# A decoder layer in float32 on one core: eight heads' products with the values in one bank, and a new order of steps

## The chip, the cores and the metric

The kernel runs on one core of one Trainium2 chip. The core has the engines PE (TensorE, matrix products and transposes), ACT (ScalarE), DVE (VectorE) and POOL (GpSimd), each with its own instruction stream, and SP (SyncE), which here issues most DMA transfers. The engines meet only at semaphores. The metric is the device time of one execution in microseconds (us).

## The reference

One decoder layer for 16 sequences of 128 tokens and 128 features, 16 heads of 8 features (`HD = 8`). Cut to what matters:

```python
# self-attention, with relative positions
attn = softmax((einsum('bhqd,bhkd->bhqk', q, k) + einsum('bhqd,qkd->bhqk', q, rk2)) / scale)
w1 = einsum('bhqk,bhkd->bhqd', attn, v)          # products with the values
w2 = einsum('bhqk,qkd->bhqd', attn, rv2)         # products with relative values
x = layernorm(x + (w1 + w2) @ Wo.T + bo)
# causal cross-attention on ctx_1024: weights @ v per head, Wo, residual, layernorm
# feed-forward: a shared expert and 8 experts (top 2 of 8, all computed and weighted), residual, layernorm
```

## The kernel before

The 16 sequences are worked in four chunks of four. For a chunk the kernel runs a list of steps. `SCHEDULE` is a text of words such as `0pv.1`: chunk 0, step `pv`, part 1. Every engine walks the same list `ORDER` in its own loop and picks from it what it has to do, so the text sets the order on each engine, on SP's queue too.

The steps of self-attention: `load` and `loadc` (input DMAs), `xT` (transpose the input), `q`, `k`, `v` (projections), `st_q`, `st_k` (the projections, split into three bf16 parts, are written to DRAM by `spread_parts` and come back stacked by head), `bias` x8 (relative-position scores, copied by ACT into the array `ST`), `p1` x8 (scores; DVE adds them to `ST` and takes maxima), `m` x2 (the row shift from the maxima, sent into the stacked queries by small DMAs), `p2` x8 (DVE subtracts the shift, ACT takes the exponential), `pv` x4 (products with the values), `w2` x4 (products with the relative values), `pvT` x4 and `w2T` x4 (back to tokens on rows), `X` (divide by the row sum), `XT`, `o`, `ln`. Cross-attention has `cT`, `ck`, `cv`, `x1T`, `cq`, `c1` x8, `cm` x2, `c2` x8, `cpv` x4, `cpvT` x4, `cX`, `cXT`, `co`, `cln`. The feed-forward part has `x2T`, `r`, `g`, `up` x18, `dn` x9, `fln`. `lrv` and `lex` load the relative values and the experts' weights once.

PSUM: steps in `S_STEPS` alternate between two double banks `ps_s`; all others, in `F_STEPS`, take the four single banks `ps_f` in turn (`take_f`, which waits until the step four uses earlier is released), and one semaphore `f_full` counts them.

The products with the values: one `pv` step does four heads. Each head's weights are 128 keys by 9 columns (8 values and a column of ones, which gives the row sum). Four heads sit in four column groups of 32 of the array (`tile_position=(0, j * QD)`), so an output bank of 128 rows holds 4 x 9 used rows. ACT copies the bank to `OT` (L818), PE transposes it in four pieces (`pvT`, L581), ACT copies the 9 columns of each head to `X` (L833).

At the start (lines 334 to 360) SP issues the loads of chunk 0, the weights, biases and the context. PE transposes chunk 0 (`xT`), the weights and the biases; the projections `q`, `k`, `v` of chunk 0 each wait for `wt_sb` at 3, by which all of self-attention's weights and the bias column are in place.

Of the kernel before, what the change touches and what calls it, by code (L numbers as in the profile page):

```python
# [98 lines left out]
2up.12 3cpvT.2 3cpv.3 2up.13 3cpvT.3 2dn.6 3cXT 2up.14 3co 2up.15 3cln 2up.16 2dn.7 2up.17 3x2T 3r 3up.0 3up.1
3up.2 2dn.8 3up.3 3g 3up.4 2fln 3up.5 3dn.0 3up.6 3dn.1 3dn.2 3up.7 3up.8 3up.9 3dn.3 3up.10 3up.11 3up.12 3dn.4  # L100
3dn.5 3up.13 3up.14 3up.15 3up.16 3up.17 3dn.6 3dn.7 3dn.8 3fln
# [17 lines left out]
def build(nc, x, ctx, sw, cw, rel_k, rel_v, router_w, router_b, sw1, sb1, sw2, sb2,  # L119
# [8 lines left out]
    F_USES = [s for s in ORDER if s[1] in F_STEPS]  # L128
# [6 lines left out]
    OT_USES = [s for s in ORDER if s[1] in ("pv", "cpv")]  # L135

    st = ExitStack()
    with st:
# [34 lines left out]
        VA = [sb(f"VA{i}", [P, NB, H, HD + 1]) for i in range(2)]  # L173
# [64 lines left out]
        stacked = {k: sem(f"stacked_{k}") for k in ("q", "k", "ck", "cq")}  # L238
        va_ready = [sem(f"va_ready{i}") for i in range(2)]
# [34 lines left out]
        def released(s):  # L274
# [9 lines left out]
                "pv": lambda: (ot_ready[0], NQ * ch + t + 1), "cpv": lambda: (ot_ready[1], NQ * ch + t + 1),  # L284
                "w2": lambda: (ow_ready, NQ * ch + t + 1),
                "pvT": lambda: (xu_ready[0], NQ * ch + t + 1), "cpvT": lambda: (xu_ready[1], NQ * ch + t + 1),
# [25 lines left out]

        def done_f(e, s):

            e.wait_ge(f_full, F_USE[s] + 1)
            return ps_f[F_USE[s] % 4]
# [14 lines left out]
        N_E = 10  # L331
# [3 lines left out]
        def _(sp):  # L335
# [23 lines left out]
            def load_relative_values():  # L359
# [739 lines left out]
```

## Time and profile before

| | |
|---|---|
| median of 3 runs | 450.4 us (450.26 to 450.72) |
| profiled execution | 451.89 us, of which the span is 450.1 us |
| PE busy | 378.3 us, 84% of the span |
| DVE busy | 303.4 us, 67% |
| ACT busy | 228.3 us, 51% |
| POOL busy | 80.0 us, 18% |
| mean granted clock of PE | 0.942 of full speed |

The profiled execution's own time is 1.8 us longer than its span, and 1.5 us longer than the median of the timed runs. "Busy" is the time in which at least one instruction of the engine runs. Matmuls are pipelined, so the mean duration of one is much longer than its share of a dense stream; what a matmul costs in such a stream is read from the length of a stretch divided by its count.

### The profile page before, as it was taken

To read this page: it belongs to the slowest core of one execution; us is meant where nothing else is said; L and a number is where in the kernel's file an instruction comes from. 1 tells how busy PE (TensorE), PEld (TensorE's weight loads), DVE (VectorE), ACT (ScalarE), POOL (GpSimd) and SP (SyncE) were. 2 spreads that over 40 slices of the span, in tenths; PEclk is the share of its full clock that TensorE was granted. 3 is DMA by queue.
4 is the path that set the end of the run, shared out by engine and by line. 5 is a ranking of instruction groups with operands and counts; after the bars stand their busy time and mean duration, and the time that the engine had idled before them with its cause. 6 is when DMAs were issued, how large, how long until landed. Compare 5 with 4: busy or idle time off the path is not lost.

```text
span 450.1 us, 11284 instructions
## 1 busy us (share of the span) xinstructions
PE 378.3 (84%) x4714; PEld 285.1 (63%) x4729; DVE 303.4 (67%) x630; ACT 228.3 (51%) x329; POOL 80.0 (18%) x92
## 2 busy tenths in 40 slices
PE   2556366974789999999999999999998989899992
PEld 1345234763566797767687976776685757566672
DVE  4246984469987679998775889998549476056324
ACT  2343046560069875326877853469944315844330
POOL 8910000020044012011131120003311202411001
PEclk9987559996989999999999999999999999999997
DMA  3261028724101360400112703010200310000100
GB/s 93 73 183 39 4 51 248 202 71 128 28 4 41 108 178 1 128 4 4 39 39 82 214 4 106 4 37 4 75 3 2 100 31 6 1 1 0 25 1 23
DMA packets 29420, 26.87 MB, mean 60 GB/s; under 512 B 12673, under 2 KB 27962, under 8 KB 28602
## 3 DMA queue, kind: packets, MB, share of 16 engines
q1 hardware_dynamic: 26042, 25.86, 20.7%
q8 instruction: 38, 0.62, 0.6%
q10 hardware_dynamic: 3136, 0.27, 0.5%
q14 instruction: 12, 0.10, 0.1%
q0 software_dynamic: 192, 0.03, 0.0%
HBM read 18.38 MB, written 7.35 MB: 57 GB/s over the span
## 4 chain that ended last, share of the span: by engine, by line
PE 54%; DVE 17%; DMA 10%; issue 6%; ACT 5%; SPq 5%; POOL 1%; POOLq 0%; DVEq 0%; ACTq 0%
PE ps_f L725 9%; PE ps_s L547 9%; PE ps_f L714 8%; PE ps_f L573 6%; PE ps_f L581 4%; DMA parts_by_head<-part 3%; PE ps_f L677 3%; PE ps_f L520 3%; DMA QS<-parts_by_head 3%; DVE ST L943 3%; PE ps_s L540 3%; DVE MX L946 3%; PE ps_s L556 2%; PE ps_f L526 2%; PE ps_s L636 2%
## 5 line engine op out<-in xcount | busy, mean ns | idle before, releaser
L547 PE MATMUL ps_s<-QS,KS 125*128 125x128 bf16 (+1 forms) x768 | 79.5, 249 | 11.9 <-DVE ST L943 6.6
L547 PEld LDWEIGHTS ps_s<-QS,KS 125*128 125x128 bf16 (+1 forms) x768 | 65.1, 106 | 34.6 <-DVE ST L943 9.0
L846 ACT ACTIVATE HT<-ps_f,hb 128x512 f32<-128x512 f32 x72 | 48.3, 688 | 74.0 <-PE ps_f L714 44.3
L725 PEld LDWEIGHTS ps_f<-w,HT 128*128 128x128 f32 x576 | 68.8, 192 | 8.1 <-issue 6.0
L725 PE MATMUL ps_f<-w,HT 128*128 128x128 f32 x576 | 72.1, 276 | 0.1
L714 PE MATMUL ps_f<-x2T,w 128*128 128x512 f32 x144 | 70.8, 602 | 1.4 <-DVE acc L1056 1.0
L488 POOL TENSOR_SCALAR_AFFINE_SELECT PC<-PC 128x1024 f32<-128x1024 f32 x32 | 34.8, 1094 | 142.2 <-ACT PC L810 142.2
L1060 DVE SCALAR_TENSOR_TENSOR acc<-ps_f,gw,acc 128x128 f32<-128x128 f32 x128 | 35.7, 341 | 21.8 <-PE ps_f L725 21.5
L810 ACT ACTIVATE PC<-ps_s 128x1024 f32<-128x1024 f32 x32 | 32.2, 1024 | 33.4 <-PE ps_s L547 30.1
L803 ACT ACTIVATE ST<-ST 128x1024 f32<-128x1024 f32 x32 | 33.9, 1061 | 28.0 <-DVE ST L974 27.6
L943 DVE TENSOR_TENSOR ST<-ps_s,ST 128x1024 f32<-128x1024 f32 x32 | 38.6, 1207 | 11.0 <-PE ps_s L547 10.9
L974 DVE TENSOR_TENSOR ST<-ps_s,ST 128x1024 f32<-128x1024 f32 x32 | 38.2, 1216 | 8.6 <-PE ps_s L556 8.2
L950 DVE TRANSPOSE_TENSOR_REDUCE MX<-ps_s 128x32 f32<-128x1024 f32 x32 | 38.7, 1232 | 3.8 <-PE ps_s L547 3.6
L946 DVE TRANSPOSE_TENSOR_REDUCE MX<-ST 128x32 f32<-128x1024 f32 x32 | 39.8, 1245 | 1.1
L494 POOL TENSOR_TENSOR ve<-mv,epst 128x4 f32<-128x4 f32 x12 | 2.4, 202 | 197.1 <-DVE mv L890 197.1
L714 PEld LDWEIGHTS ps_f<-x2T,w 128*128 128x128 f32 x144 | 24.1, 191 | 16.3 <-issue 13.9
L799 ACT COPY ST<-ps_s 128x1024 f32<-128x1024 f32 x32 | 30.9, 1025 | 6.9 <-PE ps_s L636 6.9
L540 PE MATMUL ps_s<-maskT,identb 128*128 128x512 bf16 x64 | 25.8, 402 | 8.7 <-DMA QS<-parts_by_head 5.8
L922 DVE SCALAR_TENSOR_TENSOR rest<-ps_f,bcol,part 128x512 f32<-128x512 f32 x16 | 11.9, 743 | 22.0 <-ACT part L789 22.0
L636 PE MATMUL ps_s<-QS,RK 125*128 125x64 bf16 x512 | 20.5, 197 | 5.9 <-issue 3.7
L636 PEld LDWEIGHTS ps_s<-QS,RK 125*128 125x128 bf16 x512 | 18.9, 101 | 7.9 <-issue 4.4
L556 PE MATMUL ps_s<-QS,onesr 128*128 128x512 bf16 x49 | 17.4, 422 | 6.9 <-DMA QS<-MP 4.3
(118 smaller groups left out, 525.2 us busy)
## 6 DMA issues: line engine op xcount, KB each, us to landing
parts_by_head<-part SPq DMA_DIRECT2D x16, 384.0 KB, 2.6
QS<-parts_by_head SPq DMA_DIRECT2D x24, 256.0 KB, 3.8
KS<-parts_by_head SPq DMA_DIRECT2D x24, 256.0 KB, 4.3
xin<-in_x SPq DMA_DIRECT2D x16, 64.0 KB, 2.7
cin<-in_ctx SPq DMA_DIRECT2D x4, 256.0 KB, 5.0
w<-in_L_ffn_rw SPq DMA_DIRECT2D x1, 1024.0 KB
out_x<-acc SPq DMA_DIRECT2D x16, 64.0 KB, 1.8
QS<-MP SPq DMA_DIRECT2D x32, 8.0 KB, 2.1
```

Of the source, the lines that this page charges most:

```text
L488: nc.gpsimd.affine_select(out=w, in_=w, compare_op=ALU.is_ge, fill=0.0, base=0, pattern=[[0, HB_TILE], [1, S]], channel_multiplier=-1).the ...
L540: nc.tensor.matmul(ps[:, half * BANK:(half + 1) * BANK], identb[:, :], maskT[:, :, :].broadcast_to([P, 4, S]), start=True, stop=False, ski ...
L547: last = nc.tensor.matmul(ps[:, o:o + S], KS[a][0:kd, c:c + S], queries(a, kd, h, j), start=not masked and j == 0, stop=j == NB - 1, skip_ ...
L636: last = nc.tensor.matmul(ps[:, j * HB:(j + 1) * HB], RK[0:KZ, S - 1 - q:2 * S - 1 - q], qs_q[:, :, q, :], start=True, stop=True)
L714: nc.tensor.matmul(ps[:, :], w1[:, e, f * P:(f + 1) * P], x2T[:, :], start=True, stop=True).then_inc(f_full, 1)
L725: last = nc.tensor.matmul(ps[:, b * E:(b + 1) * E], HT[n % 2][:, f, b * S:(b + 1) * S], w2[:, e, f, :], start=f == 0, stop=f == NF - 1 and ...
L846: nc.scalar.activation(HT[n % 2][:, f, :], ps[:, :], ACT.Gelu, bias=hb[:, e, f:f + 1]).then_inc(ht_ready, 1)
L943: nc.vector.tensor_tensor(by_bank(w), ps[:, :].rearrange("p (c b q) -> p c q b", b=2, q=S), by_bank(w), ALU.add).then_inc(sum_ready, 1)
L946: nc.vector.tensor_reduce(MX[0][:, t * 32:(t + 1) * 32], w.rearrange("p c (g i) -> p c g i", i=QD), AXIS.X, ALU.max, apply_transpose=True) ...
L950: nc.vector.tensor_reduce(MX[1][:, t * 32:(t + 1) * 32], ps[:, :].rearrange("p (c i) -> p c i", i=QD), AXIS.X, ALU.max, apply_transpose=Tr ...
L974: nc.vector.tensor_tensor(w, ps[:, :].rearrange("p (c i) -> p c i", i=ST_PAIR), w, ALU.add).then_inc(sc_ready, 1)
L1060: last = nc.vector.scalar_tensor_tensor(acc[:, b, :], ps[:, b * E:(b + 1) * E], gw[ch % 2][:, b, t - 1:t], acc[:, b, :], ALU.mult, ALU.add)
```

## The change

Two `pv` steps (four heads each) now share one output bank. A head's weights become 18 columns: for the first step of a pair the 9 real columns and 9 zeros, for the second 9 zeros and the 9 real columns. The second step adds into the same rows, so that each column group holds two heads. To this end `VA` is laid out with 9 zeros between the heads' 9 columns, and is filled with zeros once. The bank is taken by the first step only; ACT copies it once per pair; there are two `pvT` steps per chunk instead of four, and ACT copies each to `X` in two pieces. The same holds for `cpv` and `cpvT`. The products are counted by semaphores of their own (`pv_done`).

The experts' weights are loaded in pieces of half a tensor (`lup.0`, `lup.1`, `ldn.0`, `ldn.1`, and `lsm` for the small ones) at earlier places of the list, the relative values are extended in DRAM by a step `ext` of its own, the projections `q` and `k` of chunk 0 wait for `wt_sb` at 1 and `v` at 2, and DVE's wait for the bias rows stands at the first `v`. The list of steps is another one.

```diff
@@ SCHEDULE (its first line, of 34)
-0xT 1xT 0load 1load 0loadc 0q 0st_q 0k 0v 0st_k 0wts 0cT 0ck 0cv 0bias.0 ...
+0xT 0load 0loadc 0q 1load 0st_q 0k 0wts 0st_k 0cT 0v 0ck 0ext 1xT 0cv 0bias.0 ...
@@
-    F_USES = [s for s in ORDER if s[1] in F_STEPS]
+    F_USES = [s for s in ORDER if s[1] in F_STEPS and not (s[1] in ("pv", "cpv") and s[2] % 2)]
-        VA = [sb(f"VA{i}", [P, NB, H, HD + 1]) for i in range(2)]
+        VA = [sb(f"VA{i}", [P, VW + NB * H * 2 * VW]) for i in range(2)]
+        VA_head = [va[:, VW:VW + NB * H * 2 * VW].rearrange("p (b h d) -> p b h d", b=NB, h=H) for va in VA]
@@ def values(s, a, prob_of):
-                ps = take_f(pe, s)
+                second = s[2] % 2
+                ps = pv_bank(s) if second else take_f(pe, s)
...
-                        last = nc.tensor.matmul(ps[j * QD:j * QD + HD + 1, b * S:(b + 1) * S], VA[a][:, b, h, :],
-                                                prob_of(h, b), start=b == 0, stop=b == NB - 1,
+                        v0 = (b * H + h) * 2 * VW + (0 if second else VW)
+                        last = nc.tensor.matmul(ps[j * QD:j * QD + 2 * VW, b * S:(b + 1) * S], VA[a][:, v0:v0 + 2 * VW],
+                                                prob_of(h, b), start=not second and b == 0,
+                                                stop=bool(second) and b == NB - 1,
@@ tensor engine
-                        pe.wait_ge(wt_sb, 3)
+                        pe.wait_ge(wt_sb, 2 if what == "v" else 1)
@@ scalar engine
-                elif what in ("pv", "cpv"):
+                elif what in ("pv", "cpv") and t % 2:
...
-                    nc.scalar.copy(X[a][:, :, HQ * t:HQ * (t + 1), :],
-                                   ps[:, :].rearrange("p (a h d) -> p a h d", a=NQ, h=HQ)[:, :, :, 0:HD + 1]
-                                   ).then_inc(xu_ready[a], 1)
+                    for u in range(2):
+                        h = HQ * (2 * t + u)
+                        last = nc.scalar.copy(X[a][:, :, h:h + HQ, :],
+                                              ps[:, :].rearrange("p (a h d) -> p a h d", a=NQ, h=HQ)[:, :, :, u * VW:(u + 1) * VW])
+                    last.then_inc(xu_ready[a], 1)
@@ vector engine
+                nc.vector.memset(VA[a][:, :], 0.0).then_inc(va_zero, 1)
...
-            v.wait_ge(ld_br, 16 * 4)
@@ SP's queue: load_experts() is split
+            def load_up(half):
+                e = slice(half * NEXP // 2, (half + 1) * NEXP // 2)
+                sp.dma_start(w1[:, e, :], rw1[e].rearrange("e d h -> d e h")).then_inc(ld_e, 16)
+            def load_down(half):
...
```

Three places show how instructions move. The first is PE's queue at the start. `ident,xin` are the transposes of the input, `ident,OT` those of the weights, `TR,wT` the projections, and `ld_x1` is the load of chunk 1. Before:

```order
L598 MATMUL ps_f<-ident,OW 128x4 [waits ld_b]
L515 MATMUL ps_f<-ident,xin 128x128 [waits ld_x1]
L515 MATMUL ps_f<-ident,xin 128x128 x3
L520 MATMUL ps_f<-TR,wT 128x512 [waits xT_ready,wt_sb]
L520 MATMUL ps_f<-TR,wT 128x512 [waits c_dve,xT_ready,wt_sb]
L526 MATMUL ps_f<-wT,TR 128x128 [waits xT_ready,wt_sb]
```

And in the changed kernel:

```order
L631 MATMUL ps_f<-ident,OW 128x4 [waits ld_b]
L550 MATMUL ps_f<-TR,wT 128x512 [waits xT_ready,wt_sb] x2
L537 MATMUL ps_s<-ident,OT 128x128 [waits ld_w1]
L537 MATMUL ps_s<-ident,OT 128x128 x3
L545 MATMUL ps_f<-ident,cin 128x128 [waits c_dve,ld_c]
L545 MATMUL ps_f<-ident,cin 128x128 x3
L556 MATMUL ps_f<-wT,TR 128x128 [waits xT_ready,wt_sb]
L556 MATMUL ps_f<-wT,TR 128x128 x3
L550 MATMUL ps_f<-TR,wT 128x512 [waits rest_q,cT_ready,wt_sb]
L545 MATMUL ps_f<-ident,xin 128x128 [waits rest_k,ld_x1]
```

The first two projections no longer stand behind the transposes that wait for chunk 1's load.

The second place is PE between the last exponentials of chunk 0 and the scores of chunk 1. `ST,VA` are the products with the values, `ST,RV` those with the relative values, `ident,OT` the transposes of `pvT`. Before:

```order
L573 MATMUL ps_f<-ST,VA 9x128 x16
L677 MATMUL ps_f<-ST,RV 8x64 x64
L581 MATMUL ps_f<-ident,OT 128x128 x8
L573 MATMUL ps_f<-ST,VA 9x128 x16
L520 MATMUL ps_f<-TR,wT 128x512
L677 MATMUL ps_f<-ST,RV 8x64 x64
L526 MATMUL ps_f<-wT,TR 128x128 x4
L581 MATMUL ps_f<-ident,OT 128x128 x4
L581 MATMUL ps_f<-ident,OW 128x128 x16
```

And in the changed kernel:

```order
L605 MATMUL ps_f<-ST,VA 18x128 x16
L710 MATMUL ps_f<-ST,RV 8x64 x32
L605 MATMUL ps_f<-ST,VA 18x128 x16
L710 MATMUL ps_f<-ST,RV 8x64 x32
L550 MATMUL ps_f<-TR,wT 128x512
L710 MATMUL ps_f<-ST,RV 8x64 x32
L614 MATMUL ps_f<-ident,OT 128x128 x4
L710 MATMUL ps_f<-ST,RV 8x64 x32
L614 MATMUL ps_f<-ident,OT 128x128 x4
L614 MATMUL ps_f<-ident,OW 128x128 x16
```

There are 8 transposes of `OT` here instead of 12 (a further 4 stood ahead of these rows before); `v` of chunk 1 (`wT,TR`) comes later.

The third place is SP's queue between the keys of chunk 0 and the second row shift. `w<-in_L_ffn_rw` are the experts' weights, `QS<-MP` the shift. Before:

```order
L389 DMA parts_by_head<-part 128x3x512 [waits low_ck]
L412 DMA QS<-MP 1x128x32 [waits mp_step0]
L412 DMA QS<-MP 1x128x32
L362 DMA rel_v_by_distance<-in_L_attn_rel_v 8x41
L363 DMA rel_v_by_distance<-in_L_attn_rel_v 107x8
L364 DMA rel_v_by_distance<-in_L_attn_rel_v 107x8
L368 DMA RV<-rel_v_by_distance 128x1024 [waits ext_done]
L412 DMA QS<-MP 1x128x32 [waits mp_step0]
```

And in the changed kernel:

```order
L413 DMA parts_by_head<-part 128x3x512 [waits low_ck]
L374 DMA rel_v_by_distance<-in_L_attn_rel_v 8x41
L375 DMA rel_v_by_distance<-in_L_attn_rel_v 107x8
L376 DMA rel_v_by_distance<-in_L_attn_rel_v 107x8
L383 DMA RV<-rel_v_by_distance 128x1024 [waits ext_done]
L357 DMA cin<-in_ctx 128x4x128 [waits f_full]
L402 DMA w<-in_L_ffn_rw 128x4x256 x2
L436 DMA QS<-MP 1x128x32 [waits mp_step0]
L436 DMA QS<-MP 1x128x32
L407 DMA w<-in_L_ffn_rw 128x8x128 x2
L436 DMA QS<-MP 1x128x32 [waits mp_step0]
```

The experts' 2 MB now stand around the first shift; before they stood behind the second.

## Rows read from the trace of the kernel before

**Rows 1.** Stretches of the span: busy time of each engine in each.

```profile
core 0: us, PE busy (x) PEld busy (x) DVE busy (x) ACT busy (x) POOL busy (x), PEclk, DMA share, GB/s
37.00:60.00 23.00, 10.47 (x70) 7.47 (x71) 21.52 (x23) 1.76 (x2) 0.00 (x0) 0.55 0.08 22
...
125.00:175.00 50.00, 48.44 (x877) 38.45 (x880) 37.06 (x80) 39.83 (x59) 12.35 (x13) 0.97 0.27 75
175.00:225.00 50.00, 49.79 (x437) 37.00 (x438) 44.23 (x72) 26.29 (x36) 6.87 (x6) 1.00 0.15 39
225.00:275.00 50.00, 49.68 (x809) 40.33 (x810) 38.47 (x96) 34.90 (x54) 9.20 (x11) 1.00 0.30 84
275.00:325.00 50.00, 48.12 (x536) 35.93 (x543) 42.28 (x72) 32.41 (x42) 8.75 (x8) 1.00 0.16 43
325.00:375.00 50.00, 46.02 (x596) 33.94 (x587) 33.01 (x93) 19.83 (x34) 4.88 (x7) 1.00 0.11 31
375.00:425.00 50.00, 45.57 (x416) 33.45 (x417) 21.16 (x75) 27.66 (x39) 11.18 (x12) 1.00 0.03 7
```

**Rows 2.** Timeline of the first 30 us: start us, us, engine, line, what [idle before].

```profile
4.63 1.09 PE L515 MATMUL ps_f<-ident,xin 128*128 128x128 f32 x4 [4.63 <-DMA xin<-in_x]
...
8.06 0.27 PE L598 MATMUL ps_f<-ident,OW 4*128 4x4 f32 x1 [1.04 <-DMA OW<-in_L_xattn_bk]
...
14.95 1.11 PE L515 MATMUL ps_f<-ident,xin 128*128 128x128 f32 x4 [6.63 <-DMA xin<-in_x]
...
15.86 3.28 PE L520 MATMUL ps_f<-TR,wT 128*128 128x512 f32 x4
...
20.79 0.39 SPq L389 DMA_DIRECT2D parts_by_head<-part  x1
...
23.41 1.83 SPq L404 DMA_DIRECT2D QS<-parts_by_head  x3
...
28.92 1.87 PE L636 MATMUL ps_s<-QS,RK 125*128 125x64 bf16 x32 [3.67 <-issue]
```

**Rows 3.** Timeline, DVE's memsets at the start.

```profile
1.28 1.57 DVE L861 MEMSET ps_f<- 128x512 f32 x3
...
10.46 0.48 DVE L878 MEMSET ps_f<- 128x512 f32 x1
```

**Rows 4.** Timeline, DVE after the second row shift of chunk 0.

```profile
64.74 2.36 DVE L974 TENSOR_TENSOR ST<-ps_s,ST 128x1024 f32<-128x1024 f32 x2 [1.83 <-PE ps_s L556]
```

**Rows 5.** The page: what DMA moved, in 40 slices of the span.

```profile
GB/s 93 73 183 39 4 51 248 202 71 128 28 4 41 108 178 1 128 4 4 39 39 82 214 4 106 4 37 4 75 3 2 100 31 6 1 1 0 25 1 23
```

**Rows 6.** The chain that ended last, 68 to 110 us: start us, us, what.

```profile
68.82 2.37 DVE ST L974 x2
...
72.32 1.85 PE ps_f L677 x104
74.17 2.31 issue
...
84.59 4.78 DMA parts_by_head<-part
...
95.15 1.09 PE ps_s L547 x8
...
109.72 0.59 PE ps_s L540
```

**Rows 7.** The chain that ended last, 186 to 245 us.

```profile
186.65 1.86 PE ps_s L547 x16
...
237.88 0.44 PE ps_f L581 x4
238.32 1.02 PE ps_f L573 x32
239.34 0.59 PE ps_f L581 x4
...
243.19 1.06 PE ps_f L677 x62
```

More of the change, by code:

```diff
@@ L37 @@
 HQ = H // NQ
+NPV = NQ // 2
+VW = HD + 1
 NEXP = 8
@@ L102 @@
+3cpvT.1 2up.14 2up.15 3cXT 2up.16 3co 2dn.6 3cln 2up.17 2dn.7 3x2T 3r 3up.0 3up.1 3up.2 2dn.8 3up.3 3g 2fln 3up.4
+3up.5 3dn.0 3up.6 3dn.1 3dn.2 3up.7 3up.8 3up.9 3dn.3 3up.10 3dn.4 3up.11 3up.12 3up.13 3dn.5 3dn.6 3up.14 3up.15
+3up.16 3up.17 3dn.7 3dn.8 3fln
 """
@@ L127, in build @@
     FIRST = (0, "xT", 0)
-    F_USES = [s for s in ORDER if s[1] in F_STEPS]
+    F_USES = [s for s in ORDER if s[1] in F_STEPS and not (s[1] in ("pv", "cpv") and s[2] % 2)]
+    F_RANK = {s: n for n, s in enumerate(s for s in F_USES if s[1] not in ("pv", "cpv"))}
     S_USES = [s for s in ORDER if s[1] in S_STEPS]
@@ L134, in build @@
     TR_LAST = {u: [s for s in ORDER if s[0] == u[0] and s[1] in TR_READERS[u[1]]][-1] for u in TR_USES}
-    OT_USES = [s for s in ORDER if s[1] in ("pv", "cpv")]
+    OT_USES = [s for s in ORDER if s[1] in ("pv", "cpv") and s[2] % 2]
     st = ExitStack()
@@ L238, in build @@
         stacked = {k: sem(f"stacked_{k}") for k in ("q", "k", "ck", "cq")}
+        va_zero = sem("va_zero")
+        pv_done = [sem(f"pv_done{i}") for i in range(2)]
         va_ready = [sem(f"va_ready{i}") for i in range(2)]
@@ L311, in take_s, with pv_bank @@
             return ps_s[n % 2]
+        def pv_bank(s):
+            return ps_f[F_USE[(s[0], s[1], s[2] // 2 * 2)] % 4]
         def done_f(e, s):
-            e.wait_ge(f_full, F_USE[s] + 1)
+            if s[1] in ("pv", "cpv"):
+                e.wait_ge(pv_done[int(s[1] == "cpv")], NQ * s[0] + s[2] + 1)
+                return pv_bank(s)
+            e.wait_ge(f_full, F_RANK[s] + 1)
             return ps_f[F_USE[s] % 4]
@@ L330, in build @@
         block = st.enter_context(nc.Block())
-        N_E = 10
+        N_E = 12
         SLOT = {"q": 0, "k": 1, "ck": 2, "cq": 3}
@@ L357, in _, with extend_relative_values @@
             load_c(0)
-            def load_relative_values():
+            def extend_relative_values():
                 n_end = S - 1 - MAX_REL
@@ L378, in load_experts @@
                 sp.dma_start(ob[NEXP:NEXP + 1, :], sb2.rearrange("(o e) -> o e", o=1)).then_inc(ld_e, 16)
-                sp.dma_start(w1[:, 0:NEXP, :], rw1.rearrange("e d h -> d e h")).then_inc(ld_e, 16)
+                sp.dma_start(wr[:, :], router_w).then_inc(ld_e, 16)
                 sp.dma_start(w1[:, NEXP, :], sw1).then_inc(ld_e, 16)
-                sp.dma_start(w2[:, 0:NEXP, :, :].rearrange("p e f d -> p (e f) d"),
-                             rw2.rearrange("e (f p) d -> p (e f) d", p=P)).then_inc(ld_e, 16)
                 sp.dma_start(w2[:, NEXP, :, :], sw2.rearrange("(f p) d -> p f d", p=P)).then_inc(ld_e, 16)
-                sp.dma_start(wr[:, :], router_w).then_inc(ld_e, 16)
+            def load_up(half):
+                e = slice(half * NEXP // 2, (half + 1) * NEXP // 2)
+                sp.dma_start(w1[:, e, :], rw1[e].rearrange("e d h -> d e h")).then_inc(ld_e, 16)
+            def load_down(half):
+                e = slice(half * NEXP // 2, (half + 1) * NEXP // 2)
+                sp.dma_start(w2[:, e, :, :].rearrange("p e f d -> p (e f) d"),
+                             rw2[e].rearrange("e (f p) d -> p (e f) d", p=P)).then_inc(ld_e, 16)
             def spread_parts(ch, what):
@@ L422, in _ @@
                     stack(ch, what[3:])
+                elif what == "ext":
+                    extend_relative_values()
                 elif what == "lrv":
                     load_relative_values()
-                elif what == "lex":
-                    load_experts()
+                elif what == "lsm":
+                    load_small()
+                elif what == "lup":
+                    load_up(t)
+                elif what == "ldn":
+                    load_down(t)
                 elif what in ("m", "cm"):
@@ L682, in _ @@
                 elif what in ("pvT", "cpvT"):
-                    pe.wait_ge(ot_ready[int(what == "cpvT")], NQ * ch + t + 1)
-                    o = ot_slot((ch, what[:-1], t))
+                    pe.wait_ge(ot_ready[int(what == "cpvT")], NPV * ch + t + 1)
+                    o = ot_slot((ch, what[:-1], 2 * t + 1))
                     to_tokens(s, lambda a: OT[:, o + a * P:o + (a + 1) * P])
@@ L856, in _ @@
             for a in range(2):
-                nc.vector.memset(VA[a][:, :, :, HD:HD + 1], 1.0).then_inc(c_dve, 1)
+                nc.vector.memset(VA[a][:, :], 0.0).then_inc(va_zero, 1)
+            for a in range(2):
+                v.wait_ge(va_zero, a + 1)
+                nc.vector.memset(VA_head[a][:, :, :, HD:HD + 1], 1.0).then_inc(c_dve, 1)
             for i in range(2):
@@ L932, in _ @@
                         done_f(v, (ch - 1, "cpv" if a else "pv", NQ - 1))
-                    nc.vector.tensor_tensor(VA[a][:, :, :, 0:HD],
+                    else:
+                        v.wait_ge(ld_br, 16 * 4)
+                    nc.vector.tensor_tensor(VA_head[a][:, :, :, 0:HD],
                                             ps[:, :].rearrange("p (b h d) -> p b h d", b=NB, h=H),
```

65 lines of the change are left out of this document (31 added, 34 removed).

## Prediction, made before the changed kernel was run

> **What bounds the kernel now.** I read the busy shares of the engines first: PE 84%, DVE 67%, ACT 51%. A share is a mean over stages, so I cut the span into stretches. From 125 to 425 us PE is the bound: the six stretches leave it idle for 1.56, 0.21, 0.32, 1.88, 3.98 and 4.43 us, 12.4 us in 300 [rows 1]. A microsecond of PE work taken out there is nearly a microsecond of time, except that DVE is close behind in two stretches (44.23 and 42.28 us busy of 50) [rows 1]. In the first 125 us it is otherwise. From 37 to 60 us DVE is busy 21.52 of 23 us and PE 10.47, at a granted clock of 0.55 [rows 1]: this is chunk 0's scores, with nothing else to fill in, and DVE sets the pace. Before that nothing is busy: the first relative-position product starts at 28.92 us [rows 2]. So there are three regimes, and each part of the change has to be priced in its own.
>
> **Start of the kernel.** Before, PE has transposed chunk 0 at 4.63 us and the biases by 8.33 us, and then stands 6.63 us before the transposes of chunk 1, whose load has not landed; the projections `q` and `k` start behind them at 15.86 us [rows 2]. In the new order nothing stands between. All that `q` needs is there at 8.33 us (the bias column is the last; the weaker `wt_sb` wait frees nothing beyond it, since that transpose stands ahead of `q` on PE). From the start of the projection to the issue of the write to DRAM it took 20.79 - 15.86 = 4.93 us [rows 2], so this now comes at 13.3 us. DVE is free in time: its memset at 10.46 us ends at 10.94 [rows 3], and `q` needs DVE some 2.8 us after its start, at 11.1. Write to stack issue took 2.62 us and stack issue to first product 5.51 us [rows 2]: 13.3 + 2.6 + 5.5 = 21.4 us. The load of chunk 1 is now issued after that write. It needs four issues (some 2 us) and about 4.5 us to land, so 20.1 us; chunk 1's transposes (1.11 us [rows 2]) and `cv` (0.9 us) stand before the first product on PE, which gives 22.1 us. The later of the two counts: 28.9 - 22.1 = **6.8 us gained**. Bounds: 5 if the transfers, now closer together, slow each other, 7.5 if the load lands early.
>
> The price here is the zeroing of `VA`. PE's first transposes wait for these memsets. A memset of 512 columns takes 0.49 us [rows 3]; I scale it to 1161 columns, 1.1 us each, 2.2 us for both. DVE's first memsets then end at 5.1 us instead of 2.85, and the first transposes start half a us later than 4.63. That is covered by the biases, which PE waits for until 8.06 us [rows 2]: 0, with 0.5 us as the other end.
>
> **Chunk 0's scores, DVE-bound.** DVE's work is unchanged. It waited 1.83 us for the products that need the second row shift [rows 4]. Now the maxima of both halves come earlier among the steps and three or four `p2` parts stand after the second shift, each 1.2 us on DVE, against about 3.2 us for the shift's DMAs. I take 2 us gained (from 0 to 2.9, the latter with the smaller gaps too). Against it: 1 MB of experts' weights is issued just ahead of the second shift on SP's queue. At 248 GB/s, the most in any slice [rows 5], 1 MB is 4.2 us, and the steps between the two shifts take DVE longer (two `p1` parts and one `p2`, 6 us). So it costs nothing unless DMA is slower than that.
>
> **Chunk 0 to chunk 1.** From the first product with the relative values (72.32) to the first scores of chunk 1 (95.15) it took 22.8 us [rows 6]. Three things go. PE stood 2.31 us with no releaser in the profile [rows 6], in the stretch in which the experts' 2 MB came in; they are now loaded from 31 us on. I count it as gone. Chunk 1's keys had their write to DRAM take 4.78 us [rows 6] in the same traffic, and PE waited 0.8 us for them; now `k` is projected right after the second `w2`. And two `pvT` steps are gone, 0.5 us each (below). What is added: `XT` has one `bias` part in front of it instead of two, so PE meets the wait for `X` about 0.9 us earlier; and `v` of chunk 1 only moves within the stretch. Sum: -2.3 - 0.8 - 1.0 + 0.9 = 3.2 us gained; I take 2.6, since ACT, which copies the eight `bias` parts at about 1 us each, is the next to be waited for. Bounds: 4.3 gained, 1 lost.
>
> From there to chunk 0's cross scores it took 109.72 - 95.15 = 14.6 us [rows 6], a chain of `x1T`, `cq`, a write and a read of DRAM. DVE filled it with five parts `p1` of 2.4 us. Now it has four and the conversion of chunk 2's `q` (1.5 us), so it runs dry for some 2.9 us, of which 1.5 are repaid as work done earlier: **1.5 us lost** (0 to 4).
>
> **The PE-bound part.** Of the 16 `pvT` steps that go, 14 lie behind 125 us. Four transposes in a dense stream take 0.44 to 0.59 us [rows 7], so 14 x 0.52 = 7.3 us. The products with the values are as many as before (1024 instructions, 896 of them here) but load 18 columns instead of 9. What a wider load costs no row shows, so I bound it. Products with 8 columns of weights and 64 moving columns go at 1.06 / 62 = 17.1 ns each, those with 9 and 128 at 1.02 / 32 = 31.9 ns [rows 7]: twice the moving columns take 1.9 times as long, which leaves about 2 ns for everything that does not go with the moving columns. The load is hidden, and 9 more columns cost at most 2 ns more, 1.8 us. From the other side: a bf16 product with 128 columns of weights goes at 1.86 / 16 = 116 ns [rows 7]; if all of that were the load, it would be 0.9 ns a column, 8.2 ns for 9, and with nothing hidden 7.3 us in this part. Below nothing it cannot be, since more is loaded. I take 0.9 ns, 0.8 us, by the nearer rows. Net 6.5 us of PE work. In the stretches where DVE is at 42 to 44 of 50 us not all of it is time; I count three quarters: **5 us gained** (9 to a loss of 2).
>
> The Trainium skill speaks against this term (TensorE: Matmul & The Clock Gate, sections "LDWEIGHTS (loading the stationary operand)" and "The mechanism"): a load takes its columns divided by 1.2 GHz, and overlaps a running matmul only when it goes to another row group. All these products use all 128 rows, so by that rule the load is never hidden, and 9 more columns would cost 7.5 ns each, an estimate of 6.7 us for 896 of them. The trace disagrees so far: an exposed load of 8 or 9 columns would be 7 ns of both paces, and it shows about 2.
>
> ACT loses 16 copies of the bank. It is busy 51% and gives nothing by itself. The copies to `X` stay as many and as large. The last stage (final `dn`, `fln`) is the same work in the same order: 0.
>
> **Sum.** -6.8 - 2 - 2.6 + 1.5 - 5 = -14.9 us. The profiled execution took 451.89 us, so 437.0; it lay 1.5 us above the median of the timed runs, so I predict **435.5 us**.
>
> **Rivals.**
> 1. DVE takes over. The PE work saved behind 125 us turns into waits for DVE, which has 303.4 us of work and none less. For: 44.23 of 50 us busy [rows 1]. Against: 38.47, 33.01 and 21.16 in others. The last term is 0: 440.5 us.
> 2. The new order also closes gaps. Half of the 12.4 us idle on PE behind 125 us goes, since a step less often has to wait for one of the four banks (16 `pvT` and 16 `pv` uses fewer). For: PE is idle 3.98 and 4.43 us in stretches where DVE is not full [rows 1]. Against: those are chains through the norms and DRAM. 435.5 - 6.2 = 429.3 us.
> 3. The weight load is not hidden: 7.3 us instead of 0.8 behind 125 us and 1 us before: 443 us. Against it is the pace of the products above.
> 4. Slower: a pair holds its bank from its first step to the copy after its second, and other steps stand between. The step four uses later then waits. It decides if the wait is over 0.93 us at each of the 16 pairs (14.9 / 16); at 1.2 us each the time is 435.5 + 19.2 = 454.7 us. For it: chunk 3's second cross pair has `cX` and two `up` between its halves. Against: in a stretch of dense work the two halves are 3 to 6 us apart and the next three banks are filled with steps of 0.4 to 1.8 us, so most waits come to nothing.
> 5. The start gives nothing because the transfers of chunk 0 are themselves the bound: the loads would have to land 7 us late. 442 us.
>
> **Chances.** Forecast (431 to 439): 0.50. Rival 1: 0.16. Rival 2: 0.18. Rival 3: 0.05. Rival 5: 0.05. Rival 4: 0.04. No change, by small losses that add up: 0.02. The range for 8 in 10 is 427 to 443 us; it holds the forecast, rivals 1 and 2, and leaves out the upper part of 3, and 4. With what this kernel's timing can tell apart (about 0.2%): faster 0.94, same 0.02, slower 0.04.
>
> **What would show it.** The first `L669` product at about 22 us instead of 28.9; the first `L577` product of chunk 0 at about 30 instead of 36.9; the one of chunk 1 at about 84 instead of 95.2; the first `L570` product at 100 instead of 109.7. Products with 18 columns at 32 to 34 ns; 40 would be rival 3. PE's busy time at 368 to 371 us. If PE's idle time behind 115 us is well over 14 us, it was rival 1 (DVE fuller) or 4 (waits of `take_f` for `OT`'s copy). The forecast is wrong if the time is above 443 or below 427 us.

## The result

The changed kernel takes 437.9 us (median of 4 runs, 437.55 to 438.70); the kernel before took 450.6 us beside it (4 runs, 450.26 to 451.72). The ratio is 0.971, with a 95% interval of 0.968 to 0.973. The forecast was 435.5 us with a range of 427 to 443. The profiled execution of the changed kernel took 437.97 us, of which the span is 436.2 us.

### The profile after

The page of the changed kernel, busy time of each engine, and what DMA moved in 40 slices (for [rows 5]):

```profile
PE 373.2 (86%) x4653; PEld 277.8 (64%) x4665; DVE 303.7 (70%) x632; ACT 226.6 (52%) x317; POOL 79.9 (18%) x92
...
GB/s 94 197 124 157 100 29 158 160 111 59 7 3 53 149 98 5 130 3 4 7 39 170 148 17 95 29 5 86 29 3 2 128 6 6 2 0 2 26 0 24
```

PE lost 5.1 us of work (378.3 before), but its idle time fell by 8.8 us, from 71.8 to 63.0 us (span less busy time). So the larger part of the gain is waiting that went. DVE is as it was. Both figures are a little rough: a trace can lack records of products (4714 are in this trace of the kernel before, 4729 in that of `cols18` below, which runs the same steps), and what is lacking reads as idle time.

The timeline of the first 22 us (for [rows 2, 3]):

```profile
1.12 1.03 DVE L892 MEMSET VA<- 128x1161 f32 x1 [1.12 <-PEq L1119]
2.33 1.03 DVE L892 MEMSET VA<- 128x1161 f32 x1 [0.19 <-issue]
...
5.39 1.09 PE L545 MATMUL ps_f<-ident,xin 128*128 128x128 f32 x4 [5.39 <-DVE ps_f L899]
...
7.74 0.27 PE L631 MATMUL ps_f<-ident,OW 4*128 4x4 f32 x1 [0.41 <-DMA OW<-in_L_xattn_bk]
7.94 3.78 PE L550 MATMUL ps_f<-TR,wT 128*128 128x512 f32 x4
...
13.17 0.37 SPq L413 DMA_DIRECT2D parts_by_head<-part  x1
...
15.87 1.85 SPq L428 DMA_DIRECT2D QS<-parts_by_head  x3
...
17.68 0.66 PE L545 MATMUL ps_f<-ident,xin 128*128 128x128 f32 x4 [0.94 <-DMA xin<-in_x]
...
21.61 1.11 PE L669 MATMUL ps_s<-QS,RK 125*128 125x64 bf16 x32 [2.39 <-issue]
```

The projections start at 7.94 us instead of 15.86, the write of the queries at 13.17 instead of 20.79, the first relative-position product at 21.61 instead of 28.92. The zeroing of `VA` moved the first transposes from 4.63 to 5.39 us, and the biases, at 7.74, still came after them: that price stayed hidden.

The chain of work that ended last, from 58 to 101 us: start us, us, what (for [rows 6]):

```profile
58.34 2.37 DVE ST L1013 x2
...
67.03 3.11 DMA parts_by_head<-part
70.16 0.57 SPq L428
...
72.78 0.53 SPq L428
...
74.62 5.80 DMA parts_by_head<-part
...
81.58 4.18 DMA KS<-parts_by_head
85.76 0.05 issue
85.81 1.09 PE ps_s L577 x8
...
96.20 4.47 DMA QS<-parts_by_head
100.67 0.25 issue
100.92 0.58 PE ps_s L570
```

And the products that PE waited for in it:

```profile
64.21 1.13 PE L710 MATMUL ps_f<-ST,RV 128*8 128x64 f32 x64 [0.89 <-ACT ST L836]
75.97 0.64 PE L669 MATMUL ps_s<-QS,RK 125*128 125x64 bf16 x16 [2.10 <-issue]
85.81 1.09 PE L577 MATMUL ps_s<-QS,KS 125*128 125x128 bf16 x8 [1.85 <-DMA KS<-parts_by_head]
```

Chunk 1's keys are written to DRAM at 74.62 us, as soon as SP has issued six stacking transfers that stand ahead of them in its queue (three for chunk 1's queries from 70.16 us, three for chunk 0's cross keys from 72.78). The write takes 5.80 us, longer than the 4.78 us of before [rows 6], and PE waits 1.85 us for the keys at 85.81.

The stretch from the first cross scores to the end, before and after (columns as in [rows 1]):

```profile
109.72:450.10 340.38, 316.22 (x3845) 239.58 (x3858) 239.10 (x540) 186.31 (x269) 54.44 (x59) 0.98 0.16 43
```

```profile
100.92:436.20 335.28, 310.54 (x3794) 233.51 (x3804) 239.22 (x539) 184.16 (x256) 53.06 (x58) 0.98 0.15 41
```

PE works 5.7 us less and idles 24.7 us instead of 24.2, and the stretch is 5.1 us shorter. So most of the saved work is time; how much is read below from two traces that lack no records.

Where the 13.9 us between the two spans are, by the starts of five products:

| stretch | before | after | difference | forecast |
|---|---|---|---|---|
| to the first relative-position product | 28.92 | 21.61 | -7.3 | -6.8 |
| to the first product with the relative values | 43.40 | 42.60 | -0.8 | -2 |
| to chunk 1's first scores | 22.83 | 21.60 | -1.2 | -2.6 |
| to chunk 0's cross scores | 14.57 | 15.11 | +0.5 | +1.5 |
| to the end | 340.38 | 335.28 | -5.1 | -5 |

### The profile page after: what moved, and what is told of

The parts are those of the page before. It is cut to its first block, busy times and chain, and to the rows that moved or that the text cites. A ratio compares the mean times of both kernels' runs of the same rounds, so it can differ in the third digit from the quotient of the medians.

```text
span 436.2 us, 11109 instructions
## 1 busy us (share of the span) xinstructions
PE 373.2 (86%) x4653; PEld 277.8 (64%) x4665; DVE 303.7 (70%) x632; ACT 226.6 (52%) x317; POOL 79.9 (18%) x92
## 4 chain that ended last, share of the span: by engine, by line
PE 57%; DVE 18%; DMA 9%; ACT 6%; issue 4%; SPq 3%; POOL 1%; POOLq 0%; DVEq 0%; ACTq 0%
PE ps_f L758 12%; PE ps_f L747 12%; PE ps_s L577 9%; PE ps_f L605 4%; DMA parts_by_head<-part 3%; PE ps_s L570 3%; DVE ST L1013 3%; PE ps_f L556 3%; PE ps_s L669 3%; DVE ST L982 3%; DVE MX L985 2%; PE ps_f L614 2%; DVE MX L989 2%; PE ps_f L545 2%; DMA QS<-parts_by_head 2%
## 5 line engine op out<-in xcount | busy, mean ns | idle before, releaser
L577 PE MATMUL ps_s<-QS,KS 125*128 125x128 bf16 (+1 forms) x768 | 78.5, 247 | 12.1 <-DVE ST L982 7.0
L577 PEld LDWEIGHTS ps_s<-QS,KS 125*128 125x128 bf16 (+1 forms) x768 | 63.6, 105 | 35.5 <-issue 11.0
L758 PE MATMUL ps_f<-w,HT 128*128 128x128 f32 x576 | 71.8, 276 | 0.1
L982 DVE TENSOR_TENSOR ST<-ps_s,ST 128x1024 f32<-128x1024 f32 x32 | 38.5, 1204 | 13.9 <-PE ps_s L577 13.8
L550 PE MATMUL ps_f<-TR,wT 128*128 128x512 f32 x32 | 19.7, 707 | 3.3 <-ACT TR L794 2.3
```

The costliest lines, as they stand in the source:

```text
L577: last = nc.tensor.matmul(ps[:, o:o + S], KS[a][0:kd, c:c + S], queries(a, kd, h, j), start=not masked and j == 0, stop=j == NB - 1, skip_ ...
L758: last = nc.tensor.matmul(ps[:, b * E:(b + 1) * E], HT[n % 2][:, f, b * S:(b + 1) * S], w2[:, e, f, :], start=f == 0, stop=f == NF - 1 and ...
L982: nc.vector.tensor_tensor(by_bank(w), ps[:, :].rearrange("p (c b q) -> p c q b", b=2, q=S), by_bank(w), ALU.add).then_inc(sum_ready, 1)
```

## The experiments

Each kernel was timed in five rounds against the kernel before, in three sessions. Ratios are to the kernel before in the same session (median 451.4, 451.6 and 451.8 us).

### Is the wider weight load hidden?

Two kernels: the kernel before, with its products loading 18 and 32 columns instead of 9. The added columns are the next heads' values and fill output rows that nobody reads.

```diff
-VA[a][:, b, h, :]                       # 9 columns
+VAF[a][:, v0:v0 + VCOLS]                # VCOLS = 18, and 32; v0 = (b*H + h) * 9
```

> The kernel before, in its own order and unpaired; only each head's weights in the products with the values are 18 columns wide instead of 9 (the 9 that follow in the array are the next head's, and what they give lands in rows that nobody reads). 1024 loads get wider. My theory, that the load is hidden behind the moving columns: 0 to 1.8 us more, 450.5 to 452.4 us, and a dense step of 32 such products still takes 1.02 to 1.06 us. Rival, that such a load is never hidden (9 columns at 7.5 ns by the Trainium skill's figure, TensorE: Matmul & The Clock Gate, LDWEIGHTS): a step takes 1.26 us and the time is 456 to 458 us.

> The same with 32 columns instead of 9, the whole of a column group. If the load is hidden as long as it is shorter than the moving columns' time (31.9 ns a product): still under 1.10 us a step and 450.5 to 453 us. If it is not hidden, 23 more columns at 0.83 ns are 19 ns a product, a step takes 1.6 us, and the time is 462 to 470 us.

Measured: 451.7 us (ratio 1.000, 0.998 to 1.003) and 452.1 us (1.001, 0.999 to 1.003). A full step of products in the timeline, of 18 and of 32 columns:

```profile
245.42 1.11 PE L576 MATMUL ps_f<-ST,VA 128*18 128x128 f32 x32
```

```profile
244.64 1.13 PE L576 MATMUL ps_f<-ST,VA 128*32 128x128 f32 x32
```

With 9 columns the same step of the kernel before reads 1.10 us:

```profile
245.23 1.10 PE L573 MATMUL ps_f<-ST,VA 128*9 128x128 f32 x32
```

23 more columns in 1024 products cost at most 1.6 us by the interval. Rival 3 is gone. The Trainium skill's rule (TensorE: Matmul & The Clock Gate, "The mechanism") that a load overlaps a running product only when it goes to another row group would have charged an estimated 19 ns for each of them, by the same page's figure of columns over 1.2 GHz ("LDWEIGHTS (loading the stationary operand)"); that would be 0.6 us more on this step, and it shows 0.03. Here, where each product streams 128 float32 columns, the measurement decides against the rule.

### The start alone

The kernel before, with the changed kernel's first steps of the list and its two weaker `wt_sb` waits.

```diff
-0xT 1xT 0load 1load 0loadc 0q 0st_q 0k 0v 0st_k 0wts 0cT 0ck 0cv 0bias.0 ...
+0xT 0load 0loadc 0q 1load 0st_q 0k 0wts 0st_k 0cT 0v 0ck 1xT 0cv 0bias.0 ...
-                        pe.wait_ge(wt_sb, 3)
+                        pe.wait_ge(wt_sb, 2 if what == "v" else 1)
```

> The kernel before, unpaired and in its own order, with the start of the changed one alone: chunk 1's transposes and load behind chunk 0's projections, the projections' weaker waits. If the start is a chain that everything hangs on, the first relative-position product comes at 21.6 us instead of 28.9 and all of it reaches the end: ratio 0.984 (7.3 us). Rival, that the wait for chunk 1's load was only one of several and later transfers take it back: 0.990 to 1.000.

Measured: 444.7 us, ratio 0.985 (0.981 to 0.988), 6.8 us less. In its profile, taken of its slowest execution (446.2 us), the first relative-position product starts at 22.83 us, and the cross scores at 104.60 instead of 109.72. From the cross scores on the row reads as before:

```profile
104.60:444.50 339.90, 316.45 (x3845) 239.78 (x3858) 238.61 (x539) 186.42 (x269) 54.42 (x59) 0.98 0.16 43
```

The start is half of the whole gain, by itself, and of the 5.6 us between these two spans 5.1 are still there at the cross scores.

### The new order without the pairing

The changed kernel's list of steps, start and split loads, with `pv` and `pvT` as before (four banks, four `pvT` per chunk, 9 columns).

```diff
-... 0pv.2 0w2.0 1st_q 0st_ck 0pv.3 0w2.1 1k 0w2.2 1st_k 0pvT.0 0w2.3 0pvT.1 ...
+... 0pvT.0 0pv.2 0w2.0 1st_q 0st_ck 0pvT.1 0pv.3 0w2.1 1k 0w2.2 1st_k 0w2.3 0pvT.2 0pvT.3 ...
```

> The order, the loads and the start of the changed kernel, but products and transposes as before: one bank per step of four heads, four transposing steps (each before the step whose copy needs its half of the buffer). My theory: the order is worth what the trace shows up to the first cross scores, 8.8 us, and pairing the rest: 442.5 us (440.5 to 444.5). Rival, that the order gives all: 438 us. If the sum of the two single gains is well below the 12.7 us of both together, the new order fits only the paired kernel.

Measured: 447.7 us, ratio 0.992 (0.989 to 0.995). My expectation was 5 us too low.

```profile
101.64:444.60 342.96, 318.39 (x3860) 238.27 (x3860) 239.92 (x539) 191.25 (x270) 53.11 (x58) 0.99 0.15 41
```

To the cross scores this kernel is 8.1 us ahead of before (101.64 against 109.72), much as the changed one. Behind them it takes 2.6 us longer than before and 7.7 us longer than the changed kernel (342.96 against 340.38 and 335.28).

PE's busy time there seems to have grown by 2.2 us (318.4 against 316.2), but that is the trace: of the 48 products behind the cross scores that subtract the row shift (`QS,onesr`), the trace of before has 35, with 11.5 us, and this one all 48, with 13.6 us. Without this group PE is busy for 304.7 us in before and 304.8 us here. The fair comparison is `cols18`, the order of before with no record lacking:

```profile
108.87:449.30 340.43, 317.71 (x3858) 240.41 (x3858) 239.18 (x540) 186.53 (x269) 54.39 (x59) 0.98 0.16 43
```

Against it this kernel works 0.7 us more and idles 1.8 us more (24.57 against 22.72). As much was added before the transposes of `pvT` and `cpvT`, where PE waits 2.3 us for copies by ACT, against 0.5 in `cols18`:

```profile
L599 PE MATMUL ps_f<-ident,OT 128*128 128x128 f32 x112 | 17.0, 277 | 2.3 <-ACT HT L864 1.4 <-ACT OT L836 0.9
```

The places of these transposes were chosen for this experiment; the paired kernel has half as many and waits 0.3 us there. So the 2.6 us are for a good part a price of this experiment, and it does not split the 5 us cleanly into what the order and what the pairing gives.

### The pairing without the new order

The pairing in the order and with the start of before. The first halves were moved so that at most three other uses of the banks stand between two halves; the four banks allow no more.

```diff
-... 0p2.5 0pv.1 0p2.6 0p2.7 1q 1st_q 0pv.2 0w2.0 0w2.1 0pvT.1 0pvT.2 0st_ck 0pv.3 1k ... 1v 0pvT.3 ...
+... 0p2.5 0pv.1 0p2.6 0p2.7 1q 1st_q 0pv.2 0w2.0 0w2.1 0pvT.0 0st_ck 0pv.3 1k ... 1v 0pvT.1 ...
```

> The changed kernel with the order of before: pairs share a bank, two transposing steps instead of four, but the list of steps, the place of the experts' loads and the start are those of before (the first step of a pair is moved later where more than three uses of the four banks would stand between the halves). My theory: pairing is worth the last term of my sum, 5 us, and some 1 us ahead of 125 us: 444.5 us (442 to 447). Rival, that pairing gives nothing by itself and the order gives all: 449 to 451 us. Rival 4 of the prediction, that a pair's bank is waited for: above 451 us.

Measured: 460.5 us, ratio 1.019 (1.016 to 1.023). Slower than before, where I expected it 6 us faster. PE's groups with their idle time show why (after the bar: idle time before the group, and what ended it):

```profile
L556 PE MATMUL ps_f<-wT,TR 128*128 128x128 f32 x128 | 18.7, 293 | 3.9 <-ACT OT L851 3.8
L614 PE MATMUL ps_f<-ident,OT 128*128 128x128 f32 x64 | 10.1, 281 | 1.7 <-ACT OT L851 1.7
```

With three more groups (`dn`, `w2` and the projections) PE waits 8.6 us for ACT's copy of the shared bank (`OT L851`). In the changed kernel all such waits are 0.2 us:

```profile
L614 PE MATMUL ps_f<-ident,OT 128*128 128x128 f32 x64 | 10.2, 282 | 0.3 <-ACT OT L851 0.2
```

The waits account for 8.6 of the 16 us by which I was off; the rest I did not trace to a step.

### A shared bank held for longer

To take that mechanism by itself: the changed kernel, with the second halves of self-attention's pairs moved so that three other uses of the banks stand between the halves of 6 of these 8 pairs. In the changed kernel none of the 16 pairs has more than two.

```diff
-... 0p2.5 0pv.1 0p2.6 0p2.7 1q 0pv.2 0w2.0 1st_q 0st_ck 0pv.3 0w2.1 1k ...
+... 0p2.5 0p2.6 0p2.7 1q 0pv.1 0pv.2 0w2.0 1st_q 0st_ck 0w2.1 1k 0pv.3 ...
```

> The changed kernel with the second step of each self-attention pair moved later, so that at six of eight pairs three uses of the four banks stand between the halves (before at most two anywhere); nothing else is moved. If a pair's bank is what made pairing in the old order slow, PE now waits for ACT's copy of OT at these six pairs, 0.7 to 1.9 us each, 4 to 9 us in all: ratio to the kernel before 0.980 to 0.990, against 0.971. Rival, that the old order lost its time elsewhere: 0.971 to 0.974 and no such waits in the trace.

Measured: 451.3 us, ratio 0.999 (0.996 to 1.001). The whole gain is gone.

```profile
L710 PE MATMUL ps_f<-ST,RV 128*8 128x64 f32 x1024 | 19.7, 230 | 4.4 <-ACT OT L851 4.2 <-ACT OW L859 0.2
L605 PE MATMUL ps_f<-ST,VA 128*18 128x128 f32 x512 | 18.3, 285 | 2.6 <-ACT OT L851 2.6
L614 PE MATMUL ps_f<-ident,OT 128*128 128x128 f32 x64 | 10.9, 295 | 2.7 <-ACT OT L851 2.7
L545 PE MATMUL ps_f<-ident,Y 128*128 128x128 f32 x32 | 5.2, 283 | 4.8 <-ACT OT L851 3.4 <-DVE Y L1029 1.4
```

PE waits 12.9 us for the copy of the shared bank, where I expected 4 to 9. One wait in the timeline of PE and ACT, beside each other:

```profile
140.69 1.11 PE L605 MATMUL ps_f<-ST,VA 128*18 128x128 f32 x32
144.37 1.12 PE L605 MATMUL ps_f<-ST,VA 128*18 128x128 f32 x32 [2.57 <-ACT OT L851]
```

```profile
141.50 0.70 ACT L822 ACTIVATE part<-ps_f,bcol 128x512 bf16<-128x512 f32 x1
143.12 0.62 ACT L824 CAST part<-rest 128x512 bf16<-128x512 f32 x1 [0.92 <-DVE rest L959]
143.64 0.58 ACT L851 COPY OT<-ps_f 128x512 f32<-128x512 f32 x1
```

The second half ends, and the next product with the values takes that very bank. ACT's copy is queued behind the splitting of chunk 1's cross keys into parts, which waits for DVE. So PE pays for two other engines' queues. This is rival 4, real and priced: 13 us for pairs that are held one to three uses longer.

### Are the experts' loads to blame?

In the changed kernel DMA moves 158 and 160 GB/s in the two slices (65 to 87 us) in which chunk 1's queries and keys are written. My theory for the two waits of 2.10 and 1.85 us was that the early loads of the experts' weights crowd the queue. The changed kernel, with these loads back behind `0p2.4`:

```diff
-... 0p1.0 0lup.0 0lup.1 0p1.1 ... 0m.0 0ldn.0 0ldn.1 ... 0m.1 0lsm 0p2.1 ... 0p2.4 ...
+... 0p1.0 0p1.1 ... 0m.0 ... 0m.1 0p2.1 ... 0p2.4 0lsm 0lup.0 0lup.1 0ldn.0 0ldn.1 ...
```

> The changed kernel with the experts' loads (2.3 MB) put back to where the kernel before had them, behind 0p2.4. If these loads were what cost 2.3 + 0.8 us in the kernel before between 72 and 95 us, the first scores of chunk 1 come at 88 to 90 us instead of 85.8 and the time grows by 2 to 4 us. Rival, that DMA traffic was not to blame for PE's stop of 2.3 us: within 0.5 us.

Measured: 437.3 us, ratio 0.968 (0.964 to 0.972), the same as the changed kernel within the intervals. As the cause of the two waits the loads fall: with the loads late the waits are 0.78 and 1.27 us, together less than in either profile of the changed kernel (2.10 and 1.85; 2.46 and 1.15). But something else came back, in the middle of the products with the relative values:

```profile
67.42 0.51 PE L710 MATMUL ps_f<-ST,RV 128*8 128x64 f32 x19
69.43 0.86 PE L710 MATMUL ps_f<-ST,RV 128*8 128x64 f32 x45 [1.50 <-issue]
```

That is the stop with no releaser that before had at this place, 2.31 us [rows 6]. It is another thing than the 2.10 us wait of the changed kernel, which stands before chunk 1's relative-position products. All six kernels whose experts' loads are issued behind `0p2.4` have the stop in their profile (before, `cols18`, `cols32`, `start_only`, `pairs_old_order` and this one, 1.50 to 2.59 us); the eight profiles with the early loads have at most 0.3 us there. So the forecast named the right loads for it; how they stop PE is not shown. Chunk 1's first scores come at 87.24 us here, 0.8 and 1.4 us later than in those two profiles, and at the end nothing of it is left. The stop itself costs next to nothing, because it is off the path: DVE has chunk 1's keys split at 74.33 us, and SP's queue comes to their write only at 75.51.

### What stands ahead of the keys in SP's queue

The other theory: the keys of chunk 1 are late because chunk 0's cross keys are stacked right ahead of them. The changed kernel with one word moved:

```diff
-... 0bias.0 0bias.1 0lrv 0bias.2 ... 0w2.0 1st_q 0st_ck 0pv.3 0w2.1 1k ...
+... 0bias.0 0bias.1 0lrv 0st_ck 0bias.2 ... 0w2.0 1st_q 0pv.3 0w2.1 1k ...
```

> The changed kernel with one step moved: the stacking of chunk 0's cross keys (0st_ck, 768 KB in three transfers) directly behind the load of the relative values, in the DVE-bound stretch, instead of between chunk 1's queries and keys on SP's queue. My theory for the term that failed (from 72 to 95 us): the transfers of chunk 1's queries and keys and SP's queue are the bound there now. Then the keys' write is issued at about 72.7 instead of 74.6 us, takes 3 instead of 5.8, the wait of 1.85 us for the keys goes and the first scores of chunk 1 come at 84 instead of 85.8 us: 1.9 us less. Rival, that the traffic is no bound and the wait moves to the queries: no change (within 0.3 us).

Measured: 433.6 us, ratio 0.961 (0.957 to 0.966). Its one profiled execution was the slowest of its six (437.7 us) and shows no gain, and the changed kernel was not in that session. So it was run again, with the changed kernel beside it, and with two more orders that also project chunk 1's queries earlier.

> The changed kernel itself, in the same session as the three orders below, so that they can be compared with it: 437 to 439 us, a ratio of 0.968 to 0.973 to the kernel before. What is to be read: 2.1 us of TensorE's wait before chunk 1's first bias product and about 1.85 us before its first 1p1.

> The changed kernel with the stacking transfer of chunk 0's cross keys, 0st_ck, issued directly behind 0lrv. Theory (in the changed kernel chunk 1's keys are written late, because this transfer stands ahead of their write in SP's queue): the write of 1k starts earlier, the wait of 1.85 us for the stacked keys goes, and 1 to 4 us come off the changed kernel: 433.5 to 437, ratio 0.961 to 0.968. Rival (the start of chunk 1 is set by the next wait behind it, so the gain is eaten there): within 1 us of after_again.

Measured: 438.0 us for the changed kernel (ratio 0.969, 0.966 to 0.972), 434.3 us with the word moved (0.962, 0.959 to 0.965). The intervals do not overlap. SP's queue in it:

```profile
69.98 2.57 SPq L428 DMA_DIRECT2D QS<-parts_by_head  x3
72.60 0.58 SPq L413 DMA_DIRECT2D parts_by_head<-part  x1
76.72 1.74 SPq L428 DMA_DIRECT2D KS<-parts_by_head  x3
```

The keys' write is issued at 72.60 us instead of 74.62, takes 4.1 us instead of 5.8, and the wait before chunk 1's first scores is gone (1.85 us in the first profile of the changed kernel, 1.15 in the second). The cross scores start at 98.69 us; in the profile of the changed kernel taken beside it they start at 101.67:

```profile
98.69:432.40 333.71, 310.66 (x3804) 232.74 (x3804) 239.33 (x539) 183.99 (x256) 53.02 (x58) 0.99 0.15 42
```

```profile
101.67:437.20 335.53, 311.68 (x3804) 233.55 (x3804) 239.02 (x539) 184.19 (x256) 53.06 (x58) 0.98 0.15 41
```

Three of the 4.8 us between the spans are gained by there. This version beats both kernels.

Then the queries of chunk 1, three and six steps earlier:

```diff
-... 0p2.1 0p2.2 0p2.3 0pv.0 0p2.4 0p2.5 0pv.1 0p2.6 0p2.7 1q 0pv.2 ...
+... 0p2.1 0p2.2 0p2.3 0pv.0 0p2.4 1q 0p2.5 0pv.1 0p2.6 0p2.7 0pv.2 ...      (stck_q_early)
+... 0p2.1 1q 0p2.2 0p2.3 0pv.0 0p2.4 0p2.5 0pv.1 0p2.6 0p2.7 0pv.2 ...      (stck_q_early2)
```

> As stck_early_2, and chunk 1's projection of queries moved from behind 0p2.7 to behind 0p2.4, three steps. Theory (the 2.1 us wait before chunk 1's first bias product is for the stacked queries, whose write starts late): a further 0.5 to 2 us, 432 to 436. Rival (the projection's eviction on ScalarE or VectorE delays the softmax steps it is moved past by as much): the same as stck_early_2 or up to 1 us more.

> As stck_q_early, with the projection of queries three steps further up, behind 0p2.1. Theory: no wait for stacked queries at all, and the rest of its gain of 2.1 us: 431.5 to 435. Rival: the projection stands between the second products of the first softmax there and pushes all that follows on VectorE back by its own 1 to 2 us: 434 to 437.

Measured: 437.9 us (0.969, 0.965 to 0.973) and 438.2 us (0.969, 0.966 to 0.972): 4 us slower than without that move. Both miss the expectation, and its rival named a smaller price. DVE in the first of them:

```profile
61.08 0.75 DVE L959 SCALAR_TENSOR_TENSOR rest<-ps_f,bcol,part 128x512 f32<-128x512 f32 x1 [1.81 <-ACT part L822]
62.51 0.69 DVE L963 TENSOR_TENSOR part<-rest,part 128x512 bf16<-128x512 f32 x1 [0.68 <-ACT part L824]
63.12 3.64 DVE L1013 TENSOR_TENSOR ST<-ps_s,ST 128x1024 f32<-128x1024 f32 x3
```

The wait of 2.1 us before chunk 1's first relative-position product is gone, but splitting the queries into parts is a dialogue of DVE and ACT in which DVE works 1.4 us and waits 2.5 us. Placed among the `p2` parts, it holds them all up: the last three end at 66.8 us, where the four of the version without the move ended at 63.4. PE waits 3.60 us for them, and the cross scores start at 101.8 us again.

## Why the prediction was right, and where not

The time lay in the range, 2.4 us above the forecast. By its own steps:

- **Start, forecast -6.8, measured -7.3.** Right in mechanism and size; alone it gave 6.8 us. The first product came at 21.61 us, between the two counts (21.4 by the queries, 22.1 by the load). Chunk 1's load landed for its transposes at 17.68, not 20.1.
- **The zeroing of `VA`, forecast hidden.** Right: 1.03 us each, and the projections waited for the biases.
- **Chunk 0's scores, forecast -2, measured -0.8.** Too high: one wait for the shifted products stayed, 1.47 us before the last four `p2` parts, against 1.83 [rows 4].
- **Chunk 0 to chunk 1, forecast -2.6, measured -1.2.** The step that failed: from "PE stood 2.31 us with no releaser ... I count it as gone" and the 0.8 us wait for the keys to 3.1 us gained. The stop did go, and it comes back with the experts' loads. What I had not priced is the path right behind it, through SP's queue: the write of chunk 1's queries, their stacking, then the keys' write and stacking. On it PE now waits 2.10 us before `bias` of chunk 1 and 1.85 us for the keys, where I had put nothing. Without the three issues of `0st_ck` ahead of the keys' write, 3.7 us go.
- **To the cross scores, forecast +1.5, measured +0.5.** The sign was right, and the price smaller.
- **Behind them, forecast -5, measured -5.1.** Right in number, and the work saved was about what I had counted, but not the reason for the discount. Between the two traces that lack no record (`cols18` and the second profile of the changed kernel) PE works 6.0 us less (317.7 to 311.7; forecast 6.5) and idles 1.1 us more (22.7 to 23.9), so four fifths became time, where I had counted three quarters for a busy DVE. The waits that grew are mostly not for DVE: the products `QS,onesr` wait 3.2 us instead of 0.0, 2.3 of it for the row shift's DMAs, and the products of cross-attention with the values 2.3 us instead of 0.7, 1.4 of it for POOL's mask. What the pairing and the order each gave of this is open, for the reason given with `order_unpaired`.
- **PE's busy time, forecast 368 to 371, measured 373.2.** Missed, ahead of the cross scores. There it rose, from 62.1 to 62.7 us (61.4 to 62.8 between the two full traces), although two `pvT` steps of 0.5 us each are gone. The cause is open.
- **The offset.** I took 1.5 us off because the profiled execution of before lay above its median. That of the changed kernel lay on its median. So of the miss of 2.4 us, 1.4 are this offset and 1.0 is the terms (13.9 us between the spans, not 14.9). One profiled execution carries such a scatter.

Of the rivals, 1 (DVE takes over) and 3 (exposed load) are refuted by the rows above. So is 2 (the order closes gaps): from 125 to 425 us PE idles 11.4 us instead of 12.4, and half was to go. So is 5 (the start gives nothing): it gave 7.3. Rival 4 (the held bank) is real: I gave it its small chance from the right row, the distance between the halves. With at most two uses between them it costs 0.2 us, with three at six pairs 13 us. It decides whether the change gains at all: with the old order, even mended, the pairing loses 9 us (ratio 1.019).

## What to carry to other kernels

An accumulator that stays open over several steps is paid in banks, not in instructions: count the uses that stand between its first and last product against the banks that rotate, before counting the instructions saved. A queue in program order passes on every wait of what stands ahead, so a transfer that nobody needs yet belongs where its data are ready, not where it is read; one such word was worth 0.8%. A stop that is taken away is a gain only up to the next path that ends right behind it: look for that path before booking the stop. Moving a producer earlier is not free if it is a dialogue between two in-order engines: what it takes from them there is its work and its waits.

## What was not expected of the hardware

- From 9 to 32 columns of weights, at 128 moving float32 columns, 1024 products cost at most 1.6 us more (a step of 32 products 1.10, 1.11 and 1.13 us).
- PE stood for 1.5 to 2.6 us, with no releaser in the profile, in the middle of the products with the relative values in all six kernels that load the experts' weights just ahead of them, and for at most 0.3 us in the eight profiles that load them earlier.
- A write of 384 KB to DRAM took 3.1 us at 67 us, and 5.8 us at 74.6 us, issued right behind six stacking transfers; 4.1 us behind three.
- Two executions of one kernel (`stck_early`) lay 5 us apart, 437.7 and 432.5 us, so one profile of it showed no gain where the median showed one.
